# Attention in nine steps a group, the value matmuls of two or three steps in one run, with three buffers of exponentials

## The reference

```python
x = x + 0.5 * ffn(layernorm(x), w_gate, w_up, w_down)        # hidden 704, FP4 quantize + dequantize of inputs and weights
x = x + attention(layernorm(x), Wq, Wk, Wv, Wo)
x = x + 0.5 * ffn(layernorm(x), w_gate, w_up, w_down)
# attention, for each batch of 8 and head of 16 (T = 1024, Dh = 16)
logits = einsum('bhqd,bhkd->bhqk', q, k) * Dh ** -0.5
logits = where(causal_mask, -big, logits)
e = exp(logits - max(logits, axis=-1))
out = einsum('bhqk,bhkd->bhqd', e / sum(e), v)
```

## Time and profile before

| | |
|---|---|
| median of three runs | 2064.31 us |
| span of the profiled execution | 2063.7 us |
| PE busy | 1992.7 us (97%) |
| DVE busy | 1872.8 us (91%) |
| ACT busy | 1320.0 us (64%) |
| POOL busy | 1089.4 us (53%) |

### The profile page before, as it was taken

How to read it: one execution, slowest core, us unless ns; L and a number is a source line. 1 busy time by engine, 2 the same in 40 slices (tenths; PEclk the granted TensorE clock), 3 DMA queues, 4 the chain that set the end, 5 groups by cost and what they waited for, 6 DMA issues and landing times. The chain is left out here.

```text
span 2063.7 us, 44136 instructions
## 1 busy us (share of the span) xinstructions
PE 1992.7 (97%) x13211; PEld 1304.7 (63%) x13211; DVE 1872.8 (91%) x4691; ACT 1320.0 (64%) x2267; POOL 1089.4 (53%) x1773
## 2 busy tenths in 40 slices
PE   4999999998998999999999999999999899999999
PEld 3888888887885333333333333333328788888888
DVE  7899999998988899999999999999946899999997
ACT  4455554544774588888888888888894355555453
POOL 6788888885666112222222212222222788888885
PEclk9999999999998799999999999999999999999999
DMA  6000000001676445555545445555326000000000
GB/s 209 19 0 0 0 0 0 0 0 51 240 246 200 91 136 137 138 147 147 141 128 141 139 138 142 135 146 147 111 77 215 6 21 15 21 20 20 15 20 26
DMA packets 134841, 185.02 MB, mean 90 GB/s; under 512 B 24928, under 2 KB 76512, under 8 KB 134368
## 3 DMA queue, kind: packets, MB, share of 16 engines
q1 hardware_dynamic: 132000, 182.11, 30.3%
q10 hardware_dynamic: 2688, 1.05, 0.2%
HBM read 113.90 MB, written 85.98 MB: 97 GB/s over the span
## 5 line engine op out<-in xcount | busy, mean ns | idle before, releaser
L1832 POOL TENSOR_SCALAR_AFFINE_SELECT diag_scores<-diag_scores 128x256 f32<-128x256 f32 (+1 forms) x320 | 148.4, 464 | 695.4 <-ACT diag_scores L1797 687.5
L1334 DVE CUSTOM_DVE_ANT_0 gu_ps<-gu_ps,mask_qk 128x512 f32<-128x512 f32 (+3 forms) x676 | 334.5, 530 | 46.1 <-PE gu_ps L1319 38.0
L1319 PE MATMUL gu_ps<-k_stack,q_stack 96*128 96x512 bf16 (+3 forms) x1031 | 317.6, 340 | 9.6 <-DVE part_max L1334 3.8
L1698 PE MATMUL gu_ps<-probs,v_group 128*17 128x512 f32 (+3 forms) x3072 | 310.0, 491 | 3.0 <-ACT probs L1803 1.8
L928 PE MATMUL gu_ps<-wguT_hi,ffn_xT_hi 128*128 128x512 f32 (+1 forms) x768 | 310.4, 404 | 1.1 <-DVE ffn_xT_lo L697 1.1
L928 PE MATMUL gu_ps<-wguT_hi,ffn_xT_lo 128*128 128x512 f32 (+1 forms) x768 | 289.3, 377 | 0.0
L928 PE MATMUL gu_ps<-wguT_lo,ffn_xT_hi 128*128 128x512 f32 (+1 forms) x768 | 288.8, 376 | 0.0
L912 ACT ACTIVATE ffn_z<-xs,ffn_shift,ffn_rstd 128x256 f32 (+1 forms) x128 | 76.9, 601 | 323.9 <-POOL ffn_shift L779 323.9
L1799 ACT ACTIVATE probs<-hT_ps 128x256 f32<-128x256 f32 (+2 forms) x320 | 259.7, 812 | 11.7 <-PE hT_ps L1674 11.1
L1319 PEld LDWEIGHTS gu_ps<-k_stack,q_stack 96*128 96x128 bf16 x1031 | 94.1, 97 | 272.7 <-DVE part_max L1334 192.6
L1799 ACT ACTIVATE probs<-av_ps 128x256 f32<-128x256 f32 (+2 forms) x320 | 263.2, 822 | 0.6 <-PE av_ps L1679 0.6
(11 more groups left out here) (218 smaller groups left out, 4917.6 us busy)
## 6 DMA issues: line engine op xcount, KB each, us to landing
q_stack<-q_parts SPq DMA_DIRECT2D x192, 128.0 KB, 3.3
k_stack<-k_parts SPq DMA_DIRECT2D x192, 128.0 KB, 3.4
o_all<-o_sb SPq DMA_DIRECT2D x64, 256.0 KB
q_parts<-qkv_parts SPq DMA_DIRECT2D x32, 384.0 KB, 2.7
k_parts<-qkv_parts SPq DMA_DIRECT2D x32, 384.0 KB, 2.7
v_ones<-qkv_vst SPq DMA_DIRECT2D x16, 544.0 KB, 3.9
v_group<-v_ones SPq DMA_DIRECT2D x32, 272.0 KB, 4.2
xs<-in_L_attn_x SPq DMA_DIRECT2D x8, 1024.0 KB, 8.3
```

What stands on the lines that cost most here:

```text
L1319: mm = T.matmul(out[:, e, :], qs[0:STACK, h0 + e, t * P:(t + 1) * P], ks[0:STACK, h0 + e, c * CHUNK:c * CHUNK + w], start=True, stop=True)
L1334: last = V.tensor_tensor_reduce(out=ps[:, e * w:(e + 1) * w], in0=ps[:, e * w:(e + 1) * w], in1=mask_qk[:, CHUNK - w:CHUNK], scale=1.0, sc ...
L1698: mm = T.matmul(o_ps[h * VPAD:h * VPAD + VCOLS, CHUNK - w:CHUNK], vs[:, t, h, :], probs[:, h // 2, i % 2, h % 2, at:at + w], start=first, ...
L1832: G.affine_select(out=block_of, in_=block_of, compare_op=ALU.is_ge, fill=MASKED, base=0, pattern=[[0, 2], [0, count], [1, P]], channel_mul ...
```

## The change

- The pieces of steps 2 and 8, of 256 columns each, become one step of 512 columns, `[(0, 2), (1, 6)]`. There are nine steps. The diagonal parts of the new step 2 lie 256 columns apart (`pitch`), so its copies and exponentials have a stride.
- `probs` has three buffers (`PROBS = 3`), `i % 3`.
- The value matmuls are numbered apart from the steps (`VALUES`, ten of them: steps 0, 1, 2 for the first half, then 2 to 8 for the second) and run in four blocks: at step 3 the values of 0, 1, 2; at step 5 those of 2 (second half), 3, 4; at step 7 those of 5, 6; at step 0 of the group after it those of 7, 8. A block stands between pair A and pair B of its step.
- `MAX_STEP` is 4 instead of 5, and `turn_max` and the reciprocal move with it.
- The third buffer takes the room of the down weights: SP stores them to DRAM at the end of the first feed-forward's loads and loads them back (four transfers, 12 KB in each of 128 partitions, 1.57 MB) during the output projection, behind `send_out` and ahead of chunk 10.

```diff
@@ -117,9 +121,19 @@
         part_max = sb(top, "part_max", [P, GROUP, SEQ_TILES, 2], F32)
+        until_attention = top.enter_context(ExitStack())
+        wdT, wdT_last, wdT_last_hi = down_weights(until_attention, 0)
         until_qkv = top.enter_context(ExitStack())
         wqkvT = split_weight(until_qkv, "wqkvT", [P, 3, KD, DIM])
+
+        wd_kept = nc.dram_tensor("wd_kept", [4, P, (KH - 1) * DIM], F32, kind="Internal").ap()
+        w_kept, wd_loaded = sem("w_kept"), sem("wd_loaded")
+
+        def down_pairs(parts, last, last_hi):
+
+            return [(wd_kept[n, :, :], m[:, :, :].bitcast(F32).rearrange("p k d -> p (k d)")) for n, m in enumerate(parts)] + \
+                   [(wd_kept[n + 2, :, 0:DIM], m[:, :].bitcast(F32)) for n, m in enumerate((last, last_hi))]
         qk_parts = [nc.dram_tensor(f"{n}_parts", [3, DIM, ROWS], BF16, kind="Internal").ap() for n in "qk"]
         v_ones = nc.dram_tensor("v_ones", [BATCH, GROUPS, P, SEQ_TILES, GROUP * VCOLS], F32, kind="Internal").ap()
@@ -238,6 +252,10 @@
                 for b, last in ((4, GATE[-1]), (5, UP[-1]), (7, OUT), (6, DOWN[-1])):
                     sp.wait_ge(w_tp, last + 1)
                     load_x(b)
+                sp.wait_ge(w_lo, len(groups) + 1)
+                for kept, of in down_pairs(wdT, wdT_last, wdT_last_hi):
+                    sp.dma_start(kept, of).then_inc(w_kept, 16)
+                sp.wait_ge(w_kept, 64)
             def gpsimd(pool, part):
@@ -496,6 +515,8 @@
                 load_inverse(sp)
                 load_out(sp, 9)
                 send_out(sp)
+                for kept, of in down_pairs(*wd_again):
+                    sp.dma_start(of, kept).then_inc(wd_loaded, 16)
                 for c in range(10, OUT_CHUNKS):
                     if c == SEQ // CHUNK * (BATCH - 1):
                         sp.wait_ge(ao_stored, 32 * BATCH * GROUPS)
@@ -520,6 +541,7 @@
                     out_done(pe, "resid", OUT_CHUNKS - 2)
                 if part == OUT_PARTS - 1:
                     out_done(pe, "resid", OUT_CHUNKS - 1)
+                    pe.wait_ge(wd_loaded, 64)
             def scalar(act, part):
@@ -1437,10 +1460,21 @@
             s = att_sem
             NG = BATCH * GROUPS
-            STEPS = [[(0, 0)], [(0, 3), (0, 1)], [(0, 2)], [(1, 0)], [(1, 4)], [(1, 1)], [(1, 7), (1, 5)], [(1, 2)],
-                     [(1, 6)], [(1, 3)]]
+            STEPS = [[(0, 0)], [(0, 3), (0, 1)], [(0, 2), (1, 6)], [(1, 0)], [(1, 4)], [(1, 1)], [(1, 7), (1, 5)],
+                     [(1, 2)], [(1, 3)]]
             NS = len(STEPS)
-            HALF = 3
+            PROBS = 3
+
+
+            VALUES = [(i, j) for j in range(SEQ // CHUNK) for i in range(NS) if any(of == j for of, _ in STEPS[i])]
+            NV = len(VALUES)
+            FIRST_HALF = sum(j == 0 for _, j in VALUES)
+            read_by = {i: max(v for v in range(NV) if VALUES[v][0] == i) + 1 for i in range(NS)}
+
+
+            VALUES_AT = {3: (0, range(0, 3)), 5: (0, range(3, 6)), 7: (0, range(6, 8)), 0: (1, range(8, NV))}
+            copied_out = {FIRST_HALF: 3, NV: 0}
+            assert sorted(v for _, vs in VALUES_AT.values() for v in vs) == list(range(NV))
             def columns(j, t):
@@ -1469,8 +1524,8 @@
                 units_of[i] = [(2 if i >= MAX_STEP else 1, u) for u in range(first, round(NU * seen / sum(widths)))]
             EARLY = sum(len(units_of[i]) for i in range(MAX_STEP, NS))
-            SLOTS = {0: (0, 0, 0, 0, 0), 1: (0, 1, 0, 0, 0), 2: (1, 0, 0, 1, 0), 3: (1, 0, 1, 0, 1), 4: (1, 1, 0, 1, 1),
-                     5: (1, 1, 1, 1, 1)}
+            ORDER = {False: (0, 1, 2, 3), True: (0, 1, 4, 2, 3)}
+            SLOTS = {(False, 4): (1, 1, 1, 1), (False, 5): (2, 1, 1, 1), (True, 4): (1, 1, 1, 1, 0), (True, 5): (1, 1, 1, 1, 1)}
             BANKS = 3
@@ -1482,12 +1537,13 @@
             for i in range(NS):
                 plan[i], left = [], list(units_of[i])
-                for part, count in enumerate(SLOTS[len(left)]):
+                for part, count in zip(ORDER[i in VALUES_AT], SLOTS[i in VALUES_AT, len(left)]):
                     plan[i].append(("part", part))
                     for n in range(count):
                         plan[i].append(("entry", enter(("unit", *left.pop(0)))))
-                    if i == MAX_STEP and part == 4:
-                        plan[i].append(("entry", enter(("turn_max",))))
+                assert not left
+                if i == MAX_STEP:
+                    plan[i].append(("entry", enter(("turn_max",))))
             NE = len(ENTRIES)
             assert NE == NU + 1 and NE % BANKS == 0
             bank_of = {what: e % BANKS for e, what in enumerate(ENTRIES)}
@@ -1584,7 +1640,7 @@
                 mT = sb(ctx, "mT", [GROUP * SEQ_TILES, 2, P], BF16)
                 for r in range(1, RING):
                     ring.append(group_buffers(ctx, r))
-                probs = sb(ctx, "probs", [P, 2, 2, 2, CHUNK], F32)
+                probs = sb(ctx, "probs", [P, 2, PROBS, 2, CHUNK], F32)
                 diag_scores = sb(ctx, "diag_scores", [P, 2, 2, 2 * P], F32)
                 scores = wide
                 o_ps, turn_ps = bank[0], bank[1:1 + BANKS]
@@ -1682,22 +1738,25 @@
                             if e == 1:
                                 mm.then_inc(s[pairs[pair][0]], 1)
-                        def values(b, g, i):
+                        def values(b, g, v):
                             vs = ring[g % RING][2]
                             n = b * GROUPS + g
+                            i, half = VALUES[v]
                             for name in ("probsA", "probsB"):
                                 once(pe, name, n * NS, i + 1)
                             if i in DIAG:
                                 once(pe, "diag", n * len(DIAG), DIAG.index(i) + 1)
-                            first, last = i in (0, HALF), i in (HALF - 1, NS - 1)
+                            first, last = v in (0, FIRST_HALF), v in (FIRST_HALF - 1, NV - 1)
                             if first:
-                                once(pe, "o_sb", n * 2, i // HALF)
+                                once(pe, "o_sb", n * 2, half)
                             for j, t, at, w in pieces(i):
+                                if j != half:
+                                    continue
                                 for h in range(GROUP):
                                     mm = T.matmul(o_ps[h * VPAD:h * VPAD + VCOLS, CHUNK - w:CHUNK],
                                                   vs[:, t, h, :],
-                                                  probs[:, h // 2, i % 2, h % 2, at:at + w],
+                                                  probs[:, h // 2, i % PROBS, h % 2, at:at + w],
                                                   start=first, stop=last, skip_group_check=True)
                             mm.then_inc(s["pv"], 1)
@@ -1726,10 +1785,11 @@
                                 for what, at in plan[i]:
                                     if what == "part" and at < 4:
                                         score_head(b, g, i, at // 2, at % 2)
-                                    elif what == "part" and i:
-                                        values(b, g, i - 1)
-                                    elif what == "part" and prev:
-                                        values(*prev, NS - 1)
+                                    elif what == "part":
+                                        back, vs = VALUES_AT[i]
+                                        if not back or prev:
+                                            for v in vs:
+                                                values(*(prev if back else (b, g)), v)
                                     elif what == "entry":
                                         kind, *which = ENTRIES[at]
                                         ps = turn_ps[at % BANKS]
@@ -1788,23 +1849,35 @@
                                 if i == MAX_STEP + 3 and nxt:
                                     load_max(*nxt)
-                                d = DIAG.index(i) if i in DIAG else None
-                                first = 0 if d is None else on_diag[i] * P
+                                to = i % PROBS
                                 for pair, (sc, pr) in enumerate(pairs):
                                     once(act, sc, n * NS, i + 1)
-                                    once(act, "pv", n * NS, i - 1)
-                                    if first:
-                                        S.copy(diag_scores[:, pair, :, 0:first],
-                                               scores[pair][:, :, 0:first]).then_inc(s["taken"], 1)
-                                    S.activation(probs[:, pair, i % 2, :, first:w], scores[pair][:, :, first:w],
-                                                 ACT.Exp, scale=DH ** -0.5).then_inc(s[pr], 1)
-                                if first:
-                                    once(act, "causal", n * (2 * len(DIAG)), 2 * d + 2)
```

(60 more changed lines are left out.)

10 lines of the change are left out of this document (6 added, 4 removed).

## The result

The changed kernel takes 2155.64 us, the median of four runs (2154.58 to 2158.74); the kernel before, beside it, 2064.59 us (2063.94 to 2066.43). The ratio is 1.0441, 95% interval 1.0426 to 1.0455: slower by 4.4%, where 4.6% was forecast. The span of the profiled execution went from 2063.7 to 2152.6 us.

What follows compares the result with a forecast made beforehand. DVE, starved during long blocks by three banks, bounds a group at 25.38 + 4.56 = 29.9 us, ACT's chain at 28.9; 30.2 taken. 2.9 x 30.5 = 88.5 us plus 6 for weights gives 2159 us, range 2108 to 2196.

Steps and rivals of the forecast that it cites:

- Three banks and the block's columns set DVE's gaps: During a values block DVE has at most three banks' entries; idle at steps 3, 5, 7, 0, together 4.56 us a group.
- ACT's chain: Pair B is scored only after the block: ACT idles 6.6 us, works 22.3, 28.9 us a group; alone as rival 2119 us, 22%.
- The group: Time from reciprocal to reciprocal in attention: 30.2 us, 2.9 more than before.
- the crossing of the chains: DVE's and ACT's chains cross between steps where nearly equal, which adds a little: 30.2 us a group taken, above 29.9.
- DVE's own bound: DVE's work of 25.38 us plus 4.56 idle: a group can't take less than 29.9 us.
- Copies with a stride: ACT's strided copies and exponentials cost as those of the same size; ends: no slower, or half again as long, adding 1.4 us.
- Six blocks fewer: Ten values blocks become four, 0.24 us each: 1.44 us less on PE a group; as rival winning, 2024 us, 5%.
- Down weights: Loads ahead of chunk 10 in the output projection are uncovered: 6 us, with 0 to 9 as ends; the store costs 0.
- Third buffer: Lets ACT write on while values are late; costs nothing and gains nothing beyond making the blocks possible.
- `turn_max`: ACT's copy stands behind the diagonal exponential; DVE waits about 0.6 us in the middle of step 5, hidden by its block.
- POOL: Eight selects instead of ten in a group; idle most of the time.

Runs made afterwards that it cites:

- The first experiment: Changed kernel with each step's values run alone at the end of the next step, only steps 3 and 4 sharing a block: 2065.09 us, ratio 1.0000 to the kernel before.
- The second experiment: Changed kernel, same four blocks, with a unit put between the steps' values inside each block: 2157.79 us, ratio 1.0456 to the kernel before.
- two kernels of ten runs: One step's values to a block (only steps 3 and 4 sharing), without and with down weights loaded last: 2065.09 and 2061.13 us.

## Why the prediction was right, point by point

- *Three banks and the block's columns set DVE's gaps.* Forecast 1.22, 1.75, 0.56 and 1.03 us at steps 3, 5, 7 and 0; measured 1.12, 1.51, 0.86 and 1.09, sum 4.58 against 4.56. The two aren't counted alike: the forecast counts from the moment at which DVE could have started its next instruction, the brackets from the listed end of the last. By starts and paces the measured gaps are 1.27, 1.63, 0.94 and 1.16, sum 5.00, so the forecast is 0.4 low in all. The first experiment takes the blocks away and with them the loss, though not their length apart from their place.
- *ACT's chain.* Forecast 6.6 us idle at pair B; measured 5.9 (1.12, 1.59, 1.30 and 1.90 at steps 3, 5, 7 and 0, where 1.54, 1.87, 1.12 and 2.08 were forecast); ACT is busy 492.30 / 22 = 22.4 us of a group, 22.3 forecast. The second experiment, in which the group stays at 30 us with DVE's long gaps gone, speaks for such a chain. I had it 1 us below DVE's; by that run it is about as high.
- *The group.* 30.2 forecast, 29.91 measured. The 0.3 that I added for the crossing of the chains wasn't needed: DVE's own bound of 29.9 is the measured value. That agreement is partly luck. The bound was 25.38 busy and 4.56 idle; measured are 25.03 and 4.88, two misses of 0.3 us that cancel. And the stretches between blocks have bounds of their own, of which one runs through both readers and POOL. "No less than the sum of the gaps" held; "cut DVE and the group falls by as much", which I drew from it for the experiments, failed.
- *Copies with a stride.* The low end was right. Step 2's are the copies with gaps between their tiles. From the start of the copy to the exponential behind it is 0.48 us in the changed kernel, and the diagonal exponential is listed with 1.06; both are the values of the earlier trace rows:

```profile
1051.04 0.58 ACT L1860 COPY diag_scores<-hT_ps 128x512 f32<-128x512 f32 x1
1051.52 0.60 ACT L1862 ACTIVATE probs<-hT_ps 128x512 f32<-128x512 f32 x1
...
1053.46 1.06 ACT L1874 ACTIVATE probs<-diag_scores 128x1024 f32<-128x1024 f32 x1 [0.36 <-POOL diag_scores L1905]
```

- *Six blocks fewer, −1.44 us.* Never seen whole, since PE isn't what a group waits for. The Trainium skill, "TensorEngine Tiling (Array Packing)", PSUM Bottleneck, says that after a fourfold speedup of TensorE the copying from PSUM may become the bottleneck. Here the readers are the limit in a sharper sense: halving the readers' work makes both kernels faster, though PE's work is unchanged, and ten blocks do better than four.
- *Down weights.* 6 us forecast. Measured about 5 in the profile (9.63 against 4.67 of ACT's wait), 3.1 between the changed kernel and the one with the weights last, 3.96 between two kernels of ten runs.
- *Third buffer, `turn_max`, POOL: nothing.* The first experiment keeps the nine steps and the buffers and costs nothing, so these are right together. Two details are not: with the blocks, ACT does wait 0.41 us for the third buffer at step 5, though ahead of a longer wait for pair B that would swallow it; and the 0.6 us that DVE was to wait for `turn_max` is in none of the waits of the 700 us. The move of `turn_max` wasn't tried apart.

## What to carry to other kernels

An engine that is 97% busy needn't be the bound: here a reader was at 91%, with three banks between the two. Before work is batched on such an engine, write down for each batch the time in which it delivers nothing, and what its readers have in hand at that moment; what they lacked was lost here, since they had no slack to catch up. Make that sum for each stretch between two batches and for each chain through it, not once for the whole period: the sums here gave the right total, and the wrong answer to what would lower it.

## What the runs showed of the hardware

- Values of four heads side by side (f32, four column tiles) take 0.42 us for each 256 columns also in rows of 12 and 16 matmuls: 2.28 us for 1280 columns.
- The long wait for the weights costs PE no more in clock than the short one did. Behind its gap of 7.39 us the granted clock is 0.50, the lower of its two levels (1.2 GHz), and matmuls of 256 columns start 0.21 us apart, 12 times in a row; from 1681.73 on they start 0.12 apart. In the kernel before, behind 2.27 us of idle time, they start 0.21 apart 15 times, and as often behind the 1.83 us of the kernel with the weights last. Windows (columns as above) and two matmuls of the changed kernel:

```profile
1670.00:1675.00 5.00, 1.25 (x11) 1.04 (x9) 0.00 (x0) 0.00 (x0) 0.00 (x0) 0.98 1.03 397
1675.00:1680.00 5.00, 1.36 (x6) 1.36 (x7) 3.78 (x4) 3.53 (x4) 1.21 (x2) 0.50 0.85 284
...
1679.23 0.41 PE L534 MATMUL gu_ps<-woT_hi,out_aT_lo 128*128 128x256 f32 x1
1679.44 0.41 PE L534 MATMUL gu_ps<-woT_hi,out_aT_hi 128*128 128x256 f32 x1
```

The same place in the kernel before, with its gap of 2.27 us:

```profile
1585.00:1590.00 5.00, 2.73 (x20) 2.52 (x19) 3.61 (x4) 3.53 (x4) 1.22 (x2) 0.90 0.90 305
1590.00:1595.00 5.00, 5.00 (x35) 5.00 (x34) 4.33 (x7) 2.42 (x3) 2.73 (x6) 0.75 0.53 172
...
1590.07 0.41 PE L513 MATMUL gu_ps<-woT_hi,out_aT_hi 128*128 128x256 f32 x1
1590.28 0.41 PE L513 MATMUL gu_ps<-woT_lo,out_aT_hi 128*128 128x256 f32 x1
```

I had counted the weights as a wait alone, and the clock adds nothing to that.
